# One of each slot's two fp32 mix products written as three fp32r products of rounded and low parts

## The reference

```python
neigh = (nb * nm[None, :, None]).sum(axis=1) / nc
u = jnp.concatenate([local, neigh], axis=-1)
y_sc = jnp.tanh(u @ w1 + b1) @ w2 + b2
g = g.at[:, ci, :].set(local + y_sc[:, None] * w_y[None, :])
```

```python
q, k, v = x @ Wq + bq, x @ Wk + bk, x @ Wv + bv
attn = softmax(einsum('bnd,bmd->bnm', q, k))
out = gamma * einsum('bnm,bmc->bnc', attn, v) + inputs      # the second layer has no gamma
```

## Time and profile before

| | |
|---|---|
| runs | 4953.62, 4954.85, 4958.39 us; median 4954.85 |
| the profiled execution, its own time | 4950.95 us |
| its span | 4948.9 us |
| PE, DVE, ACT, POOL busy | 97%, 68%, 58%, 20% of the span |
| PE's granted clock over the span | 0.989 |
| mix products (line 912) | 4096 instructions, 1966.8 us busy |
| scan 0, attention, scan 1 | up to some 790 us, then to 4177 us, then to the end |

### The profile page before, as it was taken

One profiled execution on the slowest core, in us unless ns is written; L12 is line 12 of the kernel. 1 busy time (PEld: TensorE's weight loads), 2 busy tenths in 40 slices (PEclk: granted clock), 3 DMA queues, 4 the chain that ended last, 5 costly groups with the idle time before them and its releaser, 6 DMA issues.

```text
span 4948.9 us, 53360 instructions
## 1 busy us (share of the span) xinstructions
PE 4789.8 (97%) x16936; PEld 2292.7 (46%) x16936; DVE 3358.2 (68%) x5980; ACT 2886.9 (58%) x5225; POOL 985.5 (20%) x3206
## 2 busy tenths in 40 slices
PE   5999996999999999999999999999999998999997
PEld 2456653444444444444444444444444443445754
DVE  3888885666666666666666666666666663788876
ACT  1223222777777777777777777777777775223322
POOL 3454320110111111110111011101110112454431
PEclk9999997999999999999999999999999999999999
DMA  7569324111111111111111111111011413369625
GB/s 150 74 74 125 64 39 47 39 39 43 43 39 39 43 43 39 39 43 43 39 38 43 43 41 37 43 43 42 36 43 43 105 39 73 53 72 115 99 51 43
DMA packets 471686, 272.94 MB, mean 55 GB/s; under 512 B 437360, under 2 KB 438640, under 8 KB 471408
## 3 DMA queue, kind: packets, MB, share of 16 engines
q1 hardware_dynamic: 471408, 269.54, 27.2%
HBM read 135.29 MB, written 134.22 MB: 54 GB/s over the span
## 4 chain that ended last, share of the span: by engine, by line
PE 92%; DVE 4%; SPq 1%; DMA 1%; ACT 1%; issue 1%; POOL 0%; DVEq 0%; POOLq 0%; ACTq 0%
PE psum L912 37%; PE psum L885 9%; PE psum L856 9%; PE psum L837 8%; PE psum L847 8%; PE psum L947 6%; PE psum L934 6%; PE psum L898 5%; PE psum L962 3%; PE psum L923 3%; DVE shared L664 1%; DVE shared L639 1%; DVE shared L641 1%; SPq L397 1%; ACT shared L779 1%
## 5 line engine op out<-in xcount | busy, mean ns | idle before, releaser
L912 PE MATMUL psum<-shared 128*128 128x512 f32 x4096 | 1966.8, 603 | 1.3 <-DVE x L743 1.3
L701 DVE TENSOR_REDUCE top<-psum 128x1 f32<-128x1024 f32 x1024 | 1253.4, 1224 | 997.0 <-PE psum L898 997.0
L786 ACT ACTIVATE shared<-psum 128x512 f32<-128x512 f32 x2048 | 1110.9, 595 | 451.6 <-PE psum L885 447.9
L791 ACT ACTIVATE psum<-psum,top 128x1024 f32<-128x1024 f32 x1024 | 1115.1, 1089 | 362.0 <-DVE top L701 362.0
L912 PEld LDWEIGHTS psum<-shared 128*128 128x128 f32 x4096 | 718.2, 190 | 764.7 <-issue 509.1
L779 ACT ACTIVATE shared<-psum,b_col 128x320 f32<-128x320 f32 (+10 forms) x744 | 414.1, 568 | 1098.9 <-PE psum L847 1084.3
L520 POOL TENSOR_TENSOR shared<-arena 128x32 f32<-128x32 f32 (+6 forms) x1230 | 568.8, 492 | 894.3 <-PE psum L847 805.0
L534 POOL TENSOR_TENSOR ratio<-shrink,total 128x8 f32<-128x8 f32 x128 | 25.8, 201 | 2906.1 <-ACT shrink L802 2906.1
L837 PE MATMUL psum<-arena,w_own 128*128 128x320 f32 (+12 forms) x1672 | 541.5, 452 | 36.0 <-DMA arena<-x_cells 33.9
L847 PE MATMUL psum<-shared,w_sum 128*128 128x320 f32 (+10 forms) x1488 | 528.0, 477 | 49.5 <-POOL shared L520 32.7
L885 PEld LDWEIGHTS psum<-q,k 64*128 64x128 f32 x2048 | 190.7, 183 | 776.3 <-issue 677.4
(11 more groups left out here) (64 smaller groups left out, 3240.2 us busy)
## 6 DMA issues: line engine op xcount, KB each, us to landing
x<-layer_out SPq DMA_DIRECT2D x128, 512.0 KB, 3.2
layer_out<-x SPq DMA_DIRECT2D x128, 512.0 KB, 2.6
arena<-x_cells SPq DMA_DIRECT2D x8, 1520.0 KB, 12.9
layer_out<-arena SPq DMA_DIRECT2D x8, 1520.0 KB, 18.7
arena<-layer_out SPq DMA_DIRECT2D x8, 1520.0 KB, 14.0
y_cells<-arena SPq DMA_DIRECT2D x8, 1520.0 KB, 19.2
arena<-x_cells SPq DMA_DIRECT2D x4, 1504.0 KB, 17.9
layer_out<-arena SPq DMA_DIRECT2D x4, 1504.0 KB, 17.9
```

The lines of the kernel that those rows point to most:

```text
L701: nc.vector.reduce_max(top[i % 2][:, m:m + 1], rows_ps[m % 2][:], AX_X, negate=True).then_inc(row_max, 1)
L786: nc.scalar.activation(probs[u % PROBS], keys_ps[u % 2], ACT.Exp).then_inc(probs_ready, 1)
L791: nc.scalar.activation(rows_ps[m % 2][:], rows_ps[m % 2][:], ACT.Exp, bias=top[i % 2][:, m:m + 1], accum_out=total[i % 2][:, m:m + 1]).the ...
L912: nc.tensor.matmul(mix_ps, v[i % 2][:, tile(t)], probs[u % PROBS], start=(m == 0), stop=(m == MT - 1)).then_inc(mixed, 1)
```

## The change

`mix` keeps the fp32 product for even units. For odd units DVE rounds the exponentials to fp32r (`round_probs`), POOL subtracts the rounded from the full ones (`split_probs`), and PE makes three fp32r products: high values by high exponentials, low by high, high by low. The product of the two low parts is left out. Of the values, half 0 (for the even units) stays fp32, half 1 is written as its rounded part by ACT, and its low part by DVE (`low_values`). The four new pairs of buffers take 16 KB of each partition; for them the window of the arena is 48 cells smaller.

```diff
-WINDOW = 5 * CHUNK
+WINDOW = 5 * CHUNK - 48
...
-    v = shared[:2]
+    v = [shared[n][:, half(0)] for n in range(2)]
+    v_high = [sb(f"v_high{n}", [P, BANK], F32R) for n in range(2)]
+    v_low = [sb(f"v_low{n}", [P, BANK], F32R) for n in range(2)]
+    probs_high = [sb(f"probs_high{n}", [P, BANK], F32R) for n in range(2)]
+    probs_low = [sb(f"probs_low{n}", [P, BANK], F32R) for n in range(2)]
...
+        def split_probs(i, u):
+            if is_job(i):
+                n = UNITS // 2 * i + u // 2
+                pool.wait_ge(probs_rounded, n + 1)
+                nc.gpsimd.tensor_tensor(probs_low[n % 2][:], probs[u % PROBS], probs_high[n % 2][:], ALU.subtract
+                                        ).then_inc(probs_split, 1)
...
         for j in range(-2, JOBS + 1):
-            log_sums(j + 1)
+            for s in range(MT):
+                split_probs(j, 2 * s + 1)
+                if s == 5:
+                    log_sums(j + 1)
...
+        def round_probs(i, u):
+            if is_job(i):
+                n = UNITS // 2 * i + u // 2
+                dve.wait_ge(probs_ready, UNITS * i + u + 1)
+                positive(dve, mixed, 2 * (n - 2) + 2)
+                nc.vector.tensor_copy(probs_high[n % 2][:], probs[u % PROBS]).then_inc(probs_rounded, 1)
+
+        def low_values(i):
+            if is_job(i):
+                dve.wait_ge(v_rounded, i + 1)
+                nc.vector.tensor_tensor(v_low[i % 2][:], misc_ps, v_high[i % 2][:], ALU.subtract
+                                        ).then_inc(v_ready, 1)
...
+            round_probs(j, 2 * s + 1)
+            if s == 6:
+                low_values(j + 1)
...
-                positive(act, mixed, UNITS * i + u - PROBS + 1)
+                if u % 2 == 0:
+                    positive(act, mixed, UNITS * i + u - PROBS + 1)
+                else:
+                    positive(act, probs_split, UNITS // 2 * i + u // 2 - PROBS // 2 + 1)
...
-                nc.scalar.activation(v[i % 2][:, half(h)], misc_ps, ACT.Copy).then_inc(v_ready, 1)
+                if h == 0:
+                    nc.scalar.activation(v[i % 2], misc_ps, ACT.Copy).then_inc(v_ready, 1)
+                else:
+                    nc.scalar.activation(v_high[i % 2][:], misc_ps, ACT.Copy).then_inc(v_rounded, 1)
...
-            pe.wait_ge(probs_ready, UNITS * i + u + 1)
...
-            t = m % 2 * (MT // 2) + m // 2
-            nc.tensor.matmul(mix_ps, v[i % 2][:, tile(t)], probs[u % PROBS], start=(m == 0),
-                             stop=(m == MT - 1)).then_inc(mixed, 1)
+            t = tile(m // 2)
+            if m % 2 == 0:
+                pe.wait_ge(probs_ready, UNITS * i + u + 1)
+                nc.tensor.matmul(mix_ps, v[i % 2][:, t], probs[u % PROBS], start=(m == 0), stop=False
+                                 ).then_inc(mixed, 1)
+            else:
+                n = UNITS // 2 * i + u // 2
+                pe.wait_ge(probs_rounded, n + 1)
+                nc.tensor.matmul(mix_ps, v_high[i % 2][:, t], probs_high[n % 2][:], start=False, stop=False)
+                nc.tensor.matmul(mix_ps, v_low[i % 2][:, t], probs_high[n % 2][:], start=False, stop=False)
+                pe.wait_ge(probs_split, n + 1)
+                nc.tensor.matmul(mix_ps, v_high[i % 2][:, t], probs_low[n % 2][:], start=False, stop=(m == MT - 1)
+                                 ).then_inc(mixed, 1)
```

More of the change, by code:

```diff
@@ L370, in network @@
     q_raw, q_high, q_ready = sem("q_raw"), sem("q_high"), sem("q_ready")
-    v_raw, v_ready = sem("v_raw"), sem("v_ready")
+    v_raw, v_ready, v_rounded = sem("v_raw"), sem("v_ready"), sem("v_rounded")
+    probs_rounded, probs_split = sem("probs_rounded"), sem("probs_split")
     rows_ready, row_max, row_summed = sem("rows_ready"), sem("row_max"), sem("row_summed")
```

## The result

| | before | after |
|---|---|---|
| median of the runs shown beside each other | 4955.7 us | 4920.5 us (4917.7 to 4921.9) |
| span of the profiled execution | 4948.9 us | 4920.0 us |
| DVE, POOL busy | 68%, 20% | 77%, 47% |
| from the first slot of attention to the last | 3321.6 us | 3216.5 us |

The ratio is 0.9928, with a 95% interval of 0.9912 to 0.9943: faster by 35 us where 90 were forecast. 4920.5 lies inside the range (4790 to 4925), near its upper end.

What follows compares the result with a forecast made beforehand. PE's queued work was taken to bound attention, with PE and DVE linked level by level in the scans. 4951 - 219 (products) + 64 (POOL wait) + 72 (window) - 6 (earlier start) = 4862, stated as 4865 us; range 4790 to 4925.

Steps and rivals of the forecast that it cites:

- the price of an fp32r pass: PE's mix products in attention: a pass takes 0.214 us, saving 0.213 a product, -219 us over 1024 products.
- 0.214, 0.22 and 0.33: Pass prices in us: half an fp32 instruction; line 898's length less a modelled tail; the step after line 898.
- a pass of 0.22 to 0.24 (4880 to 4940): PE's mix products: each fp32r pass takes 0.22 to 0.24 us, total 4880 to 4940 us; chance 0.10.
- The wait for POOL: Attention, before the spread: unit 11's subtraction and a rounding delay POOL's log chain; PE waits 0.5 us a job, +64 us.
- Rival 1: Attention: DVE's rounding does not hold up POOL's log chain; wait 0.2 us a job, total 4818 us; chance 0.22.
- The window: Both scans, level 36: chunk 7's load queues behind chunk 5's stores, stalling 36 us each time, +72 us.
- 46 us against a landing of at most 32.5: no cost: Scans: other displaced loads, chunk 5's tightest, have seven levels or more, 46 us, before first use; no cost.
- Rival 2: Scans: the displaced loads are hidden, overtaking chunk 5's stores or needed later; total 4790 us; chance 0.12.
- The scan's earlier start: Start of scan 0: chunk loads take six issues instead of seven, so B's first late sums start earlier, -6 us.
- Nothing by throughput of DVE or POOL: Attention: added work fits idle time, DVE 4.1 of 7.8 us a job, POOL 9.4 of 22.4; no throughput cost.
- Rival 3: Attention: POOL sets the end with a dearer subtraction; at 2.2 us the total is 5048 us, slower; chance 0.07.
- rival 4: PE's mix products: an fp32r pass on 128 rows takes 0.33 us, total 5156 us, slower; chance 0.02.

Runs made afterwards that it cites:

- the halves: The changed kernel with the first two fp32r passes of each product each made as two passes of 256 columns: 4925.4 us, ratio 0.994.
- unit 11 on DVE: The changed kernel with its window back at 480 cells, and unit 11's subtraction made by DVE instead of POOL: 4794.9 us, ratio 0.9676.
- the window alone: The kernel before with only the arena's window made 48 cells smaller, products still fp32: 5019.4 us, ratio 1.0128.
- the full window: The changed kernel with the arena's window back at 480 cells, the image buffers placed inside the arena: 4851.0 us, ratio 0.9788.

## Why the prediction was right or wrong

- **The failed step is the price of an fp32r pass.** "I take 0.214, as line 898's tail is only modelled." It is 0.231 (0.216 in 16 bits). A product saves 0.858 - 3 x 0.231 = 0.165 us, not 0.213, and 1024 x 0.048 = 49 us is most of the 55 us by which the forecast missed. The rows had given three values, 0.214, 0.22 and 0.33. The middle one came straight from a row and was nearer; the low one rested on a premise of equal column rates, for which no fp32r row spoke. The mechanism, three passes on PE in place of two instructions, was right, and this term of the sum was mis-sized. The case "a pass of 0.22 to 0.24 (4880 to 4940)" is what happened; it had a chance of 0.10. The trace gives the rate with the halves. The Trainium skill, page "TensorE: Matmul & The Clock Gate", section "Back-to-back issue gap", gives columns/2.4 + 2.5 ns for a matmul alone, 216 ns at 512 columns. The 16-bit passes come out at that figure (0.216), the fp32r ones do not (0.231). For a stream of weight loads and matmuls, which these are, the same section has some 131 ns at 512 columns; no run here shows it.
- **The wait for POOL: right in place and cause, near in size.** 0.5 us a job, 64 us, was forecast; PE idles 0.40, slot 7 loses 0.453, and taking the wait away gave 56 us. The parts were off in opposite directions: the subtraction 1.278 instead of 1.17, the step that the rounding holds up 0.20 instead of 0.35. The Trainium skill, page "GPSIMD Engine Reference", section "Elementwise — side-by-side cycle accounting", gives 4497 ns for an fp32 add of 2048 columns. A quarter of it, 1.12 us, is an estimate for 512 columns with no fixed part; the measured 1.278 is above it. The Trainium skill's rule of exclusion (page "SBUF — State Buffer", section "Who interferes with whom") agrees in kind with line 556's 0.40 during the rounding: the step starts 0.08 us behind the rounding's start and ends 0.06 behind its end. Whether this rounding uses both of DVE's port pairs, as the rule asks, no run shows. Rival 1, no exclusion, has the rows against it: only steps that meet a rounding or DVE's moved subtraction are long, in the change and with unit 11 on DVE. Its time was also summed wrong: with a wait of 0.2 the sum is 4862 - 64 + 26 = 4824, not 4818.
- **The window: right in the stall, wrong in one load put at nothing.** +72 and the earlier start's -6, so +66, were forecast; 69.5 and 63 were measured, each with the earlier start in it. The stall is within 0.3 us of its forecast time. In scan 0 the stall costs more than the scan's end shows, because some 6 us come back in later levels. Part of this may be the new places of the chunks, by the 16-byte rule above: the busy time of the products with the arena falls from 541.5 to 528.0 us, and with the window alone to 528.6. That the sum still came out is partly chance: in scan 1 "46 us against a landing of at most 32.5: no cost" failed for chunk 5, whose load took 39.5 us to land and cost 6.4. Rival 2 is out.
- **The scan's earlier start: right.** -6 forecast; POOL's first late sums start at 54.63 instead of 58.90, -4.3.
- **Nothing by throughput of DVE or POOL: right**. Rival 3 needed a subtraction of 1.85 us, rival 4 a pass of 0.33.
- **Missed:** PE's 4.9 us longer wait for the first image before attention, and 4.9 us more behind the last product. Neither is the window's, since both are there with the full window too (5.4 and 4.0). What makes them was not looked into. In the kernel before with its window one place on, whose attention is the old one, they are 3.4 and 1.8, so part of them may be nothing but the difference between executions.

So 90 became 35 mostly by the 49 us for the pass. The other terms are within 8 us each of what was put down, and the two waits that the sum didn't have are some 10.

## What to carry to other kernels

Before three fp32r passes replace an fp32 product, time one pass: 3 x 0.231 against 0.858 saves 19%, not 25%, and a fourth pass loses. A helper's work in front of another engine's dependent chain costs what it has over the chain's slack, each time (here some 0.45 us a job of the subtraction's 1.28): move just that one piece (here 56 us), and look for buffers whose lifetimes do not meet before shrinking a window of loads (70 us). Lay short runs of a strided matmul operand so that they touch the fewest 16-byte groups.

## What the runs showed of the hardware that was not expected

- An fp32r matmul of 512 columns on 128 rows takes 0.231 us, 0.45 ns a column (0.46 in halves); with both operands in 16 bits 0.216, and a weight load 98 ns instead of 190.
- A moving operand of 32 or 64 short runs is slower when its runs touch more groups of 16 bytes: 10 cells 8.41 or 10.56 ns a picture, 6 cells 5.03 or 7.02.
- A POOL step of 0.20 us on 8 columns takes 0.40 when it starts inside a DVE rounding of 0.42 us from SBUF to SBUF. One of 0.24 takes 0.56 inside a DVE subtraction with both inputs in SBUF. None is longer beside DVE's row maxima, which read psum.
- DVE subtracts two 128x512 fp32 operands from SBUF in 0.70 us, POOL in 1.28; POOL writes 16 bits instead of fp32r in 1.16:
```profile
L534 POOL TENSOR_TENSOR probs_low<-shared,probs_high 128x512 bf16<-128x512 f32 x1024 | 1185.8, 1158 | 1496.7 <-DVE probs_high L755 1496.7
```
